# A macaron block on one core: attention's first maxima turned in two halves, and where the statistics of batches 3 to 7 are taken

## What is computed

```python
x = x + 0.5 * ffn(layernorm(x))          # 8 experts, top 2 of a softmax over the tokens
x = x + attn(layernorm(x))               # 16 heads of 64, one key and value head for all
x = x + 0.5 * ffn(layernorm(x))

def layernorm(x):                        # eps 1e-5
    return (x - mean(x)) / sqrt(var(x) + eps)

def attn(x):
    q = x @ Wq + bq                      # (8, 512, 16, 64)
    k, v = x @ Wk + bk, x @ Wv + bv      # (8, 512, 64)
    w = softmax(q . k / sqrt(64))        # per batch and head, over the 512 keys
    return (w . v) @ Wo + bo
```

## Time and profile before

| | |
|---|---|
| median of 3 runs | 1111.26 us (1110.81 to 1111.79) |
| the profiled execution | 1111.6 us, span of its instructions 1109.8 us |
| PE busy | 1044.3 us, 94% |
| DVE busy | 827.8 us, 75% |
| POOL busy | 693.3 us, 62% |
| ACT busy | 595.6 us, 54% |
| mean granted clock of TensorE | 0.971 of 2.4 GHz |
| first q projection | 215.44 us after the span's start |
| first exact scores | 236.51 us |
| end of quad 0's scores, start of the next projection | 247.56 us |
| turn of the normalized batch 1 | 275.59 us |

### The profile page before, as it was taken

One profiled execution on the slowest core, in us unless ns is written; L12 is line 12 of the kernel. 1 busy time (PEld: TensorE's weight loads), 2 busy tenths in 40 slices (PEclk: granted clock), 3 DMA queues, 4 the chain that ended last, 5 costly groups with the idle time before them and its releaser, 6 DMA issues.

```text
span 1109.8 us, 15621 instructions
## 1 busy us (share of the span) xinstructions
PE 1044.3 (94%) x5703; PEld 629.6 (57%) x5703; DVE 827.8 (75%) x1054; ACT 595.6 (54%) x833; POOL 693.3 (62%) x367
## 2 busy tenths in 40 slices
PE   4599999669999999999999999999999999998996
PEld 1378887345655554564555555554565455666883
DVE  9979998676766677587667669665677648699995
ACT  2235555334654564465556447467566466674561
POOL 3535665527786587578568577576568666654652
PEclk9689999869999999999999999999999999999998
DMA  5153330000101000010010001000100113512512
GB/s 157 42 179 126 132 115 20 19 0 3 39 22 39 22 21 22 21 39 22 21 40 20 21 22 39 21 22 21 37 23 22 31 32 96 190 58 80 175 52 76
DMA packets 36337, 59.35 MB, mean 53 GB/s; under 512 B 10502, under 2 KB 23847, under 8 KB 36263
## 3 DMA queue, kind: packets, MB, share of 16 engines
q1 hardware_dynamic: 36262, 58.37, 17.4%
HBM read 55.20 MB, written 2.62 MB: 52 GB/s over the span
## 4 chain that ended last, share of the span: by engine, by line
PE 84%; DVE 11%; issue 2%; ACT 1%; DMA 1%; POOL 1%; SPq 0%; ACTq 0%; DVEq 0%
PE ring L942 19%; PE ring L643 7%; PE ring L637 7%; PE ring L639 7%; PE ring L895 6%; PE ring L913 5%; PE ring L919 5%; PE ring L917 5%; PE ring L915 5%; PE ring L952 5%; PE ring L928 3%; PE ring L877 2%; PE ring L879 1%; PE ring L878 1%; PE ring L852 1%
## 5 line engine op out<-in xcount | busy, mean ns | idle before, releaser
L1609 DVE TENSOR_REDUCE mx<-ring 128x2 f32<-128x1024 f32 x256 | 299.2, 1225 | 87.8 <-PE ring L895 87.8
L536 POOL TENSOR_TENSOR sum_picksT<-sum_picksT,P_wb 128x1024 f32<-128x1024 f32 x128 | 323.0, 2524 | 18.3
L1186 ACT ACTIVATE P_wb<-ring 128x1024 f32<-128x1024 f32 x256 | 262.2, 1027 | 64.7 <-PE ring L919 35.8
L536 POOL TENSOR_TENSOR sum_picksT<-P_wb 128x1024 f32<-128x1024 f32 x64 | 153.7, 2402 | 175.4 <-ACT P_wb L1186 175.4
L573 POOL TENSOR_TENSOR R<-t,R 128x512 fp32r<-128x512 f32 x128 | 165.2, 1314 | 139.6 <-ACT R L1042 139.5
L942 PE MATMUL ring<-P_wb,t 128*64 128x512 f32 x1024 | 226.8, 595 | 0.0
L942 PEld LDWEIGHTS ring<-P_wb,t 128*64 128x64 f32 x1024 | 70.6, 137 | 132.2 <-issue 128.5
L1037 ACT ACTIVATE t<-ring,bcol 128x512 f32<-128x512 f32 x128 | 81.7, 686 | 105.5 <-PE ring L643 101.1
L1198 ACT COPY OZ<-ring 128x512 f32<-128x512 f32 x64 | 36.8, 586 | 180.5 <-PE ring L942 132.9
L637 PE MATMUL ring<-R,whi 128*128 128x512 f32 x320 | 105.3, 411 | 8.0 <-DVE R L1316 2.3
L895 PE MATMUL ring<-R 64*128 64x512 f32 x512 | 106.8, 414 | 6.2 <-DVE mx L1609 4.0
(11 more groups left out here) (211 smaller groups left out, 1413.5 us busy)
## 6 DMA issues: line engine op xcount, KB each, us to landing
P_wb<-wd SPq DMA_DIRECT2D x64, 512.0 KB, 3.9
rzb_indp<-rzd SPq DMA_DIRECT2D x64, 256.0 KB, 3.9
xs<-in_L_attn_x SPq DMA_DIRECT2D x8, 256.0 KB, 3.8
zrc<-SZ SPq DMA_DIRECT2D x128, 2.0 KB, 1.7
out<-xs SPq DMA_DIRECT2D x8, 256.0 KB, 2.5
sum_picksT<-in_L_ffn_w SPq DMA_DIRECT2D x2, 512.0 KB, 5.2
MR<-mT SPq DMA_DIRECT2D x64, 4.0 KB
t<-in_L_ffn_w SPq DMA_DIRECT2D x1, 512.0 KB, 7.2
```

Of the source, the lines that this page charges most:

```text
L536: pool.tensor_tensor(US[:, g % 2, c, :, :], first, PU[:, TPB * c + t, :, :], ALU.add).then_inc(s_ua, 1)
L1186: act.activation(PU[:, u, :, :], ring[slot(("scores", g, u))][:, :, :], ACT.Exp, scale=SCALE).then_inc(s_exp, 1)
L1609: dve.tensor_reduce(mx[:, :, u], ring[slot(("max", g, u))][:, :, :], AX.X, ALU.max).then_inc(s_max, 1)
```

## The change

Quad 0's maxima are made in another order, and turned in two halves. PE does `q_proj(0)`, the maxima of units 0 to 3 (which need only q of quad 0), `q_proj(1)`, the maximum of unit 4, `turn_half(0)` with the maxima of pair c = 0, and the maxima of units 5 to 7. `turn_half(1)` stands in quad 0's own order, behind the maximum unit 0 of quad 1 and the scores of unit 0. `half_turned` on DVE copies each half to the first eight partitions of `mT`, `place_half` on SP writes it by two DMAs. The scores of pair c wait only for the half c. PE's waits for k and v of batch 0 and for the copies of the update now stand ahead of `q_proj(0)`. Before the loop DVE takes `half_turned(1)` last.

The statistics of batches 3 to 7 and `moments(3)`, `invert(3)` leave the start. The statistics go behind `max_turned(1)` in quad 0, the moments and the inverse behind `max_turned(2)` in quad 1, ahead of `x_normal(1)`; `root(3)` on ACT goes into quad 1 between the copies of the weighted sums of the two pairs. The turn's uses of the ring are one more than before.

```diff
+        mx0 = sb("mx0", [P, PAIRS, 2, TPB])
...
+        def first_order():
+
+            return ([("q", 0, 0)] + [("max", 0, u) for u in range(TPB)] + [("q", 1, 0), ("max", 0, TPB), ("half", 0, 0)] +
+                    [("max", 0, u) for u in range(TPB + 1, UNITS)])
+
+        def quad_order(g):
+
+            todo = order(g)
+            if g == 0:
+                todo.insert(2, ("half", 0, 1))
+            return todo
...
+            def place_half(c):
+
+                wait(sp, s_mt, c + 1)
+                for par in range(2):
+                    sp.dma_start(MR[DK * par:DK * par + 1, 0, c, :].rearrange("o (j s) -> o j s", j=TPB).bitcast(F32),
+                                 mT[TPB * par:TPB * (par + 1), :].bitcast(F32)).then_inc(s_mrow, 16)
...
-                place_max_row(0)
+                for c in range(PAIRS):
+                    place_half(c)
...
                 if u == 0:
                     pe.wait_ge(s_kl, g // QUADS + 1)
-                    pe.wait_ge(s_mrow, 32 * (g + 1))
+                if t == 0:
+                    pe.wait_ge(s_mrow, 32 * (g + 2) if g else 32 * (c + 1))
...
+            def turn_half(c):
+
+                wait_drained(pe, ("half", c))
+                pe.wait_ge(s_max, TPB * (c + 1))
+                pe.transpose(ring[slot(("half", c))][0:2 * TPB, 1, 0:P], mx0[:, c, :, :].rearrange("p h j -> p (h j)"), ident[:, :]
+                             ).then_inc(s_mf, 1)
...
                 pe.wait_ge(s_wl, 4)
                 pe.wait_ge(s_uc, 3)
-                q_proj(0)
-                pe.wait_ge(s_uc, 5)
-                q_proj(1)
                 pe.wait_ge(s_uc, B - 1)
                 pe.wait_ge(s_kl, 1)
                 pe.wait_ge(s_v, 1)
-                for u in range(UNITS):
-                    scores_for_max(0, u)
-                wait_drained(pe, ("turn", -1))
-                turn_max(0, ring[slot(("turn", -1))][:, 1, :])
+                for what, g, u in first_order():
+                    if what == "q":
+                        q_proj(g)
+                    elif what == "half":
+                        turn_half(u)
+                    else:
+                        scores_for_max(g, u)
...
                 q_high(1)
-                root(3)
...
                     take_pair(g, 0)
-                    if g == MOMENTS4:
+                    if g == 1:
+                        root(3)
+                    elif g == MOMENTS4:
                         root(4)
...
+            def half_turned(c):
+                dve.wait_ge(s_mf, c + 1)
+                wait(dve, s_mrow, 32 * c)
+                dve.tensor_copy(mT[0:2 * TPB, :], ring[slot(("half", c))][0:2 * TPB, 1, 0:P]).then_inc(s_mt, 1)
...
                 k_low(0, psX[0])
-                updated_stats(TPB - 1)
                 v_bias(0, psX[1])
-                updated_stats(TPB)
                 q_low(0)
-                updated_stats(TPB + 1)
-                updated_stats(TPB + 2)
-                q_low(1)
-                updated_stats(TPB + 3).then_inc(s_stats, 1)
-                dve.wait_ge(s_stats, 4)
-                moments(3)
-                for u in range(UNITS):
-                    row_max(0, u)
-                max_turned(0, ring[slot(("turn", -1))][:, 1, :])
-                invert(3)
+                for what, g, u in first_order():
+                    if what == "max":
+                        row_max(g, u)
+                    elif what == "half":
+                        half_turned(u)
+                    elif g == 1:
+                        q_low(1)
+                half_turned(1)
...
                         max_turned(g + 1, ring[slot(("turn", g))][:, 1, :])
+                    if g == 0:
+                        for b2 in range(TPB - 1, B):
+                            ins = updated_stats(b2)
+                        ins.then_inc(s_stats, 1)
+                    elif g == 1:
+                        dve.wait_ge(s_stats, 4)
+                        moments(3)
+                        invert(3)
                     if i == 1 and b + 1 < B:
```

More of the change, by code:

```diff
@@ L300, in macaron_kernel @@
                        "v": lambda b: (s_v, b + 1), "y_back": lambda b: (s_ya, b + 1)}
[L302 to L309, removed]
+        def first_order():
[8 more added lines that the diff above has]
+            if what == "q":
+                use(("q", g), (s_ql, PAIRS * (g + 1)))
+            elif what == "half":
+                use(("half", u), (s_mt, u + 1))
+            else:
+                use_of(what, g, u)
+        for g in range(NQ):
+            for what, of, u in quad_order(g):
+                if what == "half":
+                    use(("half", u), (s_mt, u + 1))
+                else:
+                    use_of(what, of, u)
             b, i = g // QUADS, g % QUADS
@@ L312, in macaron_kernel @@
                 if what == "turn":
-                    use(("turn", g), *([(s_sz, g)] if g else []), *([(s_mt, g + 2)] if g + 1 < NQ else []))
+                    use(("turn", g), *([(s_sz, g)] if g else []), *([(s_mt, g + 3)] if g + 1 < NQ else []))
                 elif what == "weigh":
@@ L470, in late_weights @@
                         load_wb(1, p, e)
+            def place_half(c):
[3 more added lines that the diff above has]
+                                 mT[TPB * par:TPB * (par + 1), :].bitcast(F32)).then_inc(s_mrow, 16)
             def place_max_row(g):
-                wait(sp, s_mt, g + 1)
+                wait(sp, s_mt, g + 2)
                 for par in range(2):
@@ L976, in attention @@
                 pe.wait_ge(s_v, 1)
-                for u in range(UNITS):
-                    scores_for_max(0, u)
-                wait_drained(pe, ("turn", -1))
-                turn_max(0, ring[slot(("turn", -1))][:, 1, :])
+                for what, g, u in first_order():
+                    if what == "q":
+                        q_proj(g)
+                    elif what == "half":
+                        turn_half(u)
+                    else:
+                        scores_for_max(g, u)
                 for g in range(NQ):
                     b, i = g // QUADS, g % QUADS
-                    for what, of, u in order(g):
-                        if what == "max":
+                    for what, of, u in quad_order(g):
+                        if what == "half":
+                            turn_half(u)
+                        elif what == "max":
                             scores_for_max(of, u)
@@ L1608, in row_max @@
                 dve.wait_ge(s_s, UNITS * g + u + 1)
-                dve.tensor_reduce(mx[:, :, u], ring[slot(("max", g, u))][:, :, :], AX.X, ALU.max).then_inc(s_max, 1)
+                dve.tensor_reduce(mx[:, :, u] if g else mx0[:, u // TPB, :, u % TPB], ring[slot(("max", g, u))][:, :, :], AX.X, ALU.max).then_inc(s_max, 1)
+            def half_turned(c):
+                dve.wait_ge(s_mf, c + 1)
+                wait(dve, s_mrow, 32 * c)
+                dve.tensor_copy(mT[0:2 * TPB, :], ring[slot(("half", c))][0:2 * TPB, 1, 0:P]).then_inc(s_mt, 1)
             def max_turned(g, bank):
-                dve.wait_ge(s_mf, g + 1)
-                wait(dve, s_mrow, 32 * g)
+                dve.wait_ge(s_mf, g + 2)
+                wait(dve, s_mrow, 32 * (g + 1))
                 dve.tensor_copy(mT[:, :], bank[0:2 * UNITS, 0:P]).then_inc(s_mt, 1)
```

## The result

The changed kernel takes 1109.45 us in the median against 1111.97 of the kernel before, timed together: a ratio of 0.9978 with a 95% interval of 0.9969 to 0.9987, so 2.5 us or 0.22% faster. One of the twelve launches of the changed kernel took 2937.6 us; it counts as slow and has no part in the ratio. Timed again on another occasion it gave 0.9979 (0.9970 to 0.9989). The profiled run took 1108.95 us with a span of 1107.2.

The account below looks back on a forecast made before the run. PE bounds most of the kernel, DVE the start of attention. A start gain of 4.7 us less 2.65 us lost in quad 1 gives -2.05, a median of 1109.3 us, range 1106.6 to 1112.2.

Parts of the forecast that it names:

- the sum: Whole kernel: start -4.7 and quad 1 +2.65 give -2.05 us, 1109.6 on the profiled run, 1109.3 for the median.
- Part 1: Start of attention: first scores 7.4 us earlier, of which 4.7 us remain at the projection behind quad 0.
- The clock: Quad 0's scores: TensorE's clock rises after some 4 us without a hole, leaving a start gain of 4.7 us.
- The bounds of 3.2 and 6.2: Start's gain in us: 6.2 if the clock is up by 234, 3.2 if it stays low 3 us longer.
- Part 2: Quad 0's weighted sums: twenty statistics, 3.9 us, fit DVE's 5.9 us hole at no cost, 2 us to spare.
- Part 3: Quad 1: stalled moments, root and inverse make batch 1's turn 1.65 us late; with the exponential's delay, 2.65 us in all.
- The wait for the table: Quad 1 into quad 2: table load delays the first exponential; PE's third scores 0.9 us late, plus 0.1 slow restart.
- B: Clock rises before the second scores (+1.5) or quad 1's seven moments lose their stalls (+1.0): 1107.8 us; chance 0.15.
- C: TensorE's clock falls at the end of quad 1, with 3.9 us of work at the low level: 1110.8 us; chance 0.18.
- D: Clock falls at the end of quad 1, drawn out, 3.0 us lost: 1112.3 us, slower than before; chance 0.10.
- E: Drain behind the table load before quad 2's first exponential, PE 1.4 us later: 1110.7 us; chance 0.03.
- F: Start: first scores early, but PE waits for banks; quad 0 ends at most 2 us earlier: 1111.5 us; chance 0.04.

Follow-up runs that it names:

- the two of the cures together without spare work: Changed kernel with maximum first, early table, moments split between start and quad 0: 1109.31 us; with maximum first, all moments in quad 0, early table: 1105.16 us.

## Why the prediction held, and where it was off

The forecast was 1109.3 us and -2.05 us on the profiled run. The median is 1109.45, the ratio 2.5 us. That the medians agree within 0.15 us is partly luck: the kernel before had 1111.26 in its three first launches and 1111.97 in twelve, and the gain is 0.4 larger than the sum. The steps below are what the prediction is judged by.

**Part 1, up to the first scores.** The first projection was put 0.7 us later, against 4.71 us behind the turn of batch 0 before; it is 5.62, so 0.9: the v bias took 0.42 us where the sum had 0.32, and PE began 0.26 behind it where the sum had 0.1. The first scores were put 7.4 us earlier; 25.78 us became 18.49, 7.3. The second scores were put 3.8 us behind the first, and stand 3.88 behind them, by the named path: PE's turn of the second half behind the first scores, DVE idle for 1.59 us, then a maximum. The experiment with the maximum first took just that wait away.

**The clock was the mis-sized term.** The prediction let it rise some 4 us after work had become unbroken (3.9 us behind the second scores, at 236.8). In the first profile it took 5.4, and the start gained 3.9 us, not 4.7; in the second 3.0, and it gained 5.0. The bounds of 3.2 and 6.2 held both. That the hole ahead of the second scores itself delays the rise was in the sum, from the earlier trace rows, and the kernel with the maximum first bears it out; what a removed hole would give back was not worked out.

**Part 2** was at no cost, and the rows bear it: twenty statistics in 3.94 us, then 2.04 us of idle time, POOL's additions not lengthened (2.4 us each, as forecast).

**Part 3.** Moments of 6.3 us were forecast and 6.3 are there (264.31 to 270.61), with the stalled call and one more to each gap between POOL's additions. The turn of batch 1 was to be 1.65 us late; it is 1.70. The wait for the table was to cost 1.0; it is 0.96. The run with the early table took away 1.0, that term whole; the run with the moments elsewhere took away 1.04 of the 1.70, where 1.05 was expected, the rest being the root's path and what one stall still cost.

**The rivals.** B's free moments chain did not occur, nor did its early clock: the rise came behind the second scores in both profiles, by 5.4 and 3.0 us. C and D are refuted: the clock is 1.00 in both windows between 271 and 279, though PE was busy 2.48 of 4 us. E is refuted: the load ends at 275.56 and the exponential starts at 275.58; there is no time for the drain that the page ScalarE: Activation LUTs of the Trainium skill, section What ACT_TABLE_LOAD costs, states. F is refuted by the stretches: quad 0 ended 3.9 and 5.0 us earlier, not 2.

The chances put 0.60 on a change within 0.2% and 0.33 on faster. The measured 0.22% lies on that border, its interval on both sides of it. On which side a launch falls is not decided by the clock's moment at the start alone: the second profile has the earlier rise and the shorter start, and yet the longer span (1107.8 against 1107.2 us), by the parts ahead of the start and at the end. Of the changed kernel's first launches the four with a mean clock of 0.977 or 0.978 took 1109.1 to 1111.9 us, the seven with 0.974 or 0.975 took 1108.6 to 1109.8.

## What to carry to other kernels

Work taken off a bound engine at the start of a stage must be followed to its first reader: here half to two thirds of what quad 0 gained was lost again in quad 1, as a chain across three engines that nobody had to wait for as long as it stood early. Put small dependent VectorE operations where GpSimd is idle, not where VectorE is; and put a table switch where ScalarE waits for another engine, by a call of one column if need be. Where a stage begins with waits on TensorE, ask what a hole costs twice: by itself, and by the clock that it keeps low behind it.

## What the runs showed of the hardware

How many small calls slip through went with POOL's gap. Between its additions of exponentials, each of which waits for the one before and starts 0.14 us behind it, the stalled call and one more went through (2.26, 0.19, 2.23 us); between its updates, which follow each other without a gap, only the stalled one (1.18 to 1.26 each, five times). These are two places, and the calls also differ in width (28 and 8 columns), so the gap as the cause is argued and not shown. A stall is thus the length of POOL's instruction, and seven calls of 0.2 us cost 6.3 us in the one place and 6.5 in the other.

A hole of 0.8 us in PE's work at the low clock put off the rise to the high one: 6.8 to 9.3 us behind the first scores in the four profiles with it, and 7.5 us in one with a hole of 1.1, against 3.4 to 6.3 us in the five without a hole (before, the moved statistics alone, the maximum first, and the two of the cures together without spare work). The closest pair is 232.4 and 235.9, from first scores at 229.03 and 229.07. At the high level a stretch with 2.48 of 4 us busy did not bring it down.

A table load did not cost more than its own 1.28 us here: the exponential started 0.02 us behind its end. It is also issued ahead of the wait of the exponential that needs it. In the changed kernel's start the load ran at 222.23 and the exponential at 230.46.
